# Attention scores in crossed 64x64 tiles by blocks of 64, the causal mask added in PSUM, and the value product in two blocks per half

## The chip, the cores and the metric

One core of a Trainium2 chip runs the whole program. The metric is the device time of one execution in microseconds, lower is better; the time given for a kernel is the median of its runs.

## What is computed

The input is 16 sequences of 512 tokens with 128 features. Three layers follow one another: a mixture of experts, an attention layer, and the same mixture of experts again. Only the attention layer changes here:

```python
q = (x @ Wq + bq).reshape(Bb, Ss, H, HD)      # H = 16 heads of HD = 8
k = (x @ Wk + bk).reshape(Bb, Ss, H, HD)
v = (x @ Wv + bv).reshape(Bb, Ss, H, HD)
scores = jnp.einsum('bthd,bshd->bhts', q, k) / jnp.sqrt(jnp.asarray(HD, x.dtype))
scores = scores + alibi[None]
scores = jnp.where(causal[None, None], -jnp.inf, scores)
attn = jax.nn.softmax(scores, axis=-1)
out = jnp.einsum('bhts,bshd->bthd', attn, v).reshape(Bb, Ss, Dd)
return out @ Wo + bo
```

Here x is layer-normalised first, and the result is added to it.

## The kernel before

**Stages.** `macaron` runs `moe_layer`, `attention` and `moe_layer`. In `attention` each engine has its own program, and all of them follow one order, written out in `walk` (L773): a step b handles sequence b, and at the same time takes the maxima of sequence b+1, the projections of b+2 and the normalisation of b+3. Steps run from -3 to 16; `all_steps` (L763) writes steps -3 to 1 and 12 to 16 out and puts steps 2 to 11 into a loop of two steps each. Step -1 takes maxima only, and step 15 has no maxima.

**Operands.** q and k are split into bf16 parts and stacked, so that one head is 64 rows of `q_st` and `k_st`: head parts, rows for the position term, a row that carries the shift (minus the maximum) and rows that build the mask. A pair of heads (a side a and a side b) fills the rows 0 to 63 and 64 to 127.

**A step before.** It has four groups g of four heads each, all of one side of a half (half `g // 2`, side `g % 2`), and a group has 11 places n:

- *Max unit* (`take_max_scores`, L871): the scores of 128 queries of one head (or of 2 or 4 heads, where few keys lie ahead) against the keys up to them, in one of three PSUM banks `max_ps`. L884 makes the far keys (51 rows deep) and L887 the diagonal block of 128 keys with the mask (64 rows deep). VectorE's `find_max` (L1093) reduces each bank to `neg_max`. A bank is used again when its reduction is done.
- *Exp unit* (`take_exp_scores`, L906, 10 a group): the transposed scores, 128 keys by the queries from them on, in one of three banks `exp_ps`. They lie in the other row half than the max unit's. ScalarE's `exponentiate` (L986) writes `probs`, of which there are two.
- *Mask* (L1058): GpSimd sets the forbidden quarter of `probs` to zero, 4 instructions a group.
- *Values* (`weigh_values`, L922): after places 3, 5, 7 and 9 the products of the previous group's `probs` with v, for keys 0, 1, 2 and 3 of 128, four heads in four column quarters of `pv_ps`, in float32. After the second group of a half, ScalarE copies `pv_ps` to `oT` (L997).
- *Side work*, all through one bank `side_ps`, each waiting until the one before is read: project_q, project_k (L937), project_v (L941), turn_h (L935), the shifts (L947), turn_o0 and turn_o1 (L961, then the divisions on VectorE, L1143 and L1145), turn_o (L952) and output (L955, added on VectorE, L1135). ScalarE copies q and k (L1010); VectorE copies v (L1127).

Where the side work stands is a table by group and place:

```python
SIDE_WORK = [
    {2: "project_q", 4: "shift_hi", 8: "project_k"},
    {1: "turn_o1", 6: "project_v"},
    {1: "turn_o", 6: "shift_lo", 10: "output"},
    {1: "turn_o0", 8: "turn_h"},
]
PV_AFTER = {3: 0, 5: 1, 7: 2, 9: 3}
```

The SP queue stores the parts of q and k (L827), stacks them (L835, L841; the first half waits for the exponentials of the first half two sequences earlier) and places the shifts (L848).

Of the kernel before, what the change touches and what calls it, by code (L numbers as in the profile page):

```python
# [19 lines left out]
P = 128  # L20
# [24 lines left out]
GROUPS = H // 4  # L45
# [21 lines left out]
class Consts:  # L67


    def __init__(self, nc, ctx):  # L70
# [5 lines left out]
        b16 = np.concatenate([bf16_parts(a, 1)[0] for a in (eye, before, np.ones((P, P)))], axis=1)  # L76
# [19 lines left out]
        self.ones_b = b[:, 2 * P:3 * P]  # L96

# [31 lines left out]
def moe_layer(nc, tag, x, consts, Wr, We, x_in=None, out=None, ahead=None):  # L129
# [7 lines left out]
    with ExitStack() as ctx:  # L137
# [289 lines left out]
        def _(dve):  # L427
# [131 lines left out]
            for e in (2, 3):  # L559
# [6 lines left out]
    {2: "project_q", 4: "shift_hi", 8: "project_k"},  # L566
    {1: "turn_o1", 6: "project_v"},
    {1: "turn_o", 6: "shift_lo", 10: "output"},
    {1: "turn_o0", 8: "turn_h"},
# [3 lines left out]
PREPARE = {(0, 5): "split_q0", (0, 6): "split_q1", (0, 7): "split_q2", (0, 8): "split_q3",  # L573
           (0, 10): "split_k0", (1, 0): "split_k1", (1, 1): "split_k2", (1, 2): "split_k3", (2, 5): "add_bias"}
NORMALISE = {(2, 0): "statistics", (2, 1): "aggregate", (2, 2): "add_eps", (2, 3): "take_root", (2, 7): "shift_mean",
             (2, 8): "normalise0", (2, 9): "normalise1", (2, 10): "normalise2", (3, 0): "normalise3"}
PV_AFTER = {3: 0, 5: 1, 7: 2, 9: 3}
MAX_UNITS = 11
EXP_UNITS = 10
MASK_UNITS = 4  # L580

def max_unit(n):

    return [(3, [0]), (3, [1]), (3, [2]), (3, [3]), (2, [0]), (2, [1]), (2, [2]), (2, [3]),
            (1, [0, 1]), (1, [2, 3]), (0, [0, 1, 2, 3])][n]  # L590


def exp_unit(n):

    if n < 4:
        return [(n, 0, 0)]
    if n < 8:
        return [(n - 4, 1, 0), (n - 4, 3, 3 * P)]
    return [(2 * (n - 8), 2, 0), (2 * (n - 8) + 1, 2, 2 * P)]


class AttentionOperands:


    def __init__(self, nc, ctx, consts, Wq, bq, Wk, bk, Wv, bv, Wo, bo):
# [11 lines left out]
        self.v = [sb(f"v{i}", [P, T, PAIRS, 2, VW]) for i in range(2)]  # L617
# [20 lines left out]
    def set_v(self, pool):  # L638

        for i in range(2):  # L640
            self.nc.gpsimd.memset(self.v[i][:], 0.0).then_inc(self.v_set, 1)
        pool.wait_ge(self.v_set, 2)
        for i in range(2):
            for ab in range(2):
                one = ab * VS + HD
                self.nc.gpsimd.memset(self.v[i][:, :, :, ab, one:one + 1], 1.0).then_inc(self.v_set, 1)


def attention(nc, x, consts, ops):
# [12 lines left out]
    with ExitStack() as ctx:  # L662
# [21 lines left out]
        neg_max = both(lambda i: sb(f"neg_max{i}", [P, 2, 2, PAIRS // 2, T], BF16))  # L684
        shift = sb("shift", [T * H // 2, P], BF16)
        probs = both(lambda i: sb(f"probs{i}", [P, EXP_UNITS, S]))
# [27 lines left out]
        SHIFT_DMAS = 1  # L714
# [4 lines left out]
        masked = sem("masked")  # L719
# [5 lines left out]
        NM, NE, NK = GROUPS * MAX_UNITS, GROUPS * EXP_UNITS, GROUPS * MASK_UNITS  # L725
        HALVES = GROUPS // 2

# [45 lines left out]
        def walk(b, par, half, on_max=None, on_exp=None, on_pv=None, on_side=None, on_prepare=None):  # L773

            for g in range(GROUPS):
                for n in range(MAX_UNITS):
                    if on_max and there(b + 1):
                        on_max(b + 1, 1 - par, half + par, g, n)
                    if on_exp and n < EXP_UNITS and there(b):
                        on_exp(b, par, half, g, n)  # L780
                    if on_prepare and (g, n) in PREPARE and there(b + 2):
                        on_prepare(b + 2, par, half + 1, PREPARE[g, n])
                    if on_prepare and (g, n) in NORMALISE and there(b + 3):
                        on_prepare(b + 3, 1 - par, half + par + 1, NORMALISE[g, n])
# [36 lines left out]
        def _(sp):  # L821
# [22 lines left out]
            def place_shift(b, par, half, hf):  # L844

                sp.wait_ge(side_read, use(b if hf else b - 1, "shift_hi" if hf else "shift_lo"))
                pairs = slice(hf * PAIRS // 2, (hf + 1) * PAIRS // 2)
                sp.dma_start(q_st[par][SHIFT_ROW:SHIFT_ROW + SIDE + 1:SIDE, pairs, :],  # L848
                             shift[:]).then_inc(shift_in[par][hf], DMA)
# [16 lines left out]
        def _(pe):  # L866
            def take_max_scores(b, par, half, g, n):

                i, heads = max_unit(n)
                m = g * MAX_UNITS + n  # L870
                if n == 0 and g in (0, 2):  # L871

                    pe.wait_ge(stack_in[par][g // 2], half * (STACK_DMAS * DMA) + STACK_DMAS * DMA)
# [5 lines left out]
                width = (i + 1) * P  # L879
                half_at, ab = g // 2, 1 - g % 2  # L880
                for c, hh in enumerate(heads):
                    r, at, low = 4 * half_at + hh, c * width, ab * SIDE
                    if i > 0:
                        nc.tensor.matmul(max_ps[m % RING][:, at:at + width - P],  # L884
                                         q_st[par][low:low + FAR_ROW, r, i * P:(i + 1) * P],
                                         k_st[par][low:low + FAR_ROW, r, 0:width - P], start=True, stop=True)
                    mm = nc.tensor.matmul(max_ps[m % RING][:, at + width - P:at + width],  # L887
                                          q_st[par][low:low + SIDE, r, i * P:(i + 1) * P],
                                          k_st[par][low:low + SIDE, r, width - P:width], start=True, stop=True)
                mm.then_inc(max_out, 1)  # L890

            def take_exp_scores(b, par, half, g, n):

                m = g * EXP_UNITS + n
                if n == 0 and g in (0, 2):

                    pe.wait_ge(shift_in[par][g // 2], half * (SHIFT_DMAS * DMA) + SHIFT_DMAS * DMA)
# [5 lines left out]
                low = (g % 2) * SIDE  # L903
                for hh, j, c in exp_unit(n):
                    r = 4 * (g // 2) + hh
                    mm = nc.tensor.matmul(exp_ps[m % RING][:, c:c + S - j * P],  # L906
                                          k_st[par][low:low + FINE_ROW, r, j * P:(j + 1) * P],
                                          q_st[par][low:low + FINE_ROW, r, j * P:S], start=True, stop=True)
                mm.then_inc(exp_out, 1)

            def weigh_values(b, par, g, j):

                half_at, ab = divmod(g, 2)
                if j == 0:
                    pe.wait_ge(masked, b * NK + (g + 1) * MASK_UNITS)
                    if ab == 0 and (g > 0 or after(b, 0)):
                        pe.wait_ge(pv_read, b * HALVES + half_at)
                    if g == 0:
                        pe.wait_ge(side_read, use(b - 1, "project_v"))
                for hh in range(4):  # L920
                    n, c = next((n, c) for n in range(EXP_UNITS) for h, jj, c in exp_unit(n) if (h, jj) == (hh, j))
                    mm = nc.tensor.matmul(pv_ps[VW * hh:VW * (hh + 1), j * P:S], v[par][:, j, 4 * half_at + hh, ab, :],  # L922
                                          probs[g % 2][:, n, c:c + S - j * P], start=(ab == 0 and j == 0),
                                          stop=(ab == 1 and j == T - 1))
                if j == T - 1:
                    mm.then_inc(pv_out, 1)

            def side(b, par, half, what):
# [10 lines left out]
                elif what == "project_v":  # L939
                    for t in range(T):  # L940
                        mm = nc.tensor.matmul(side_ps[:, t * P:(t + 1) * P], hT[1 - par][:, t * P:(t + 1) * P],  # L941
                                              w["wv"][:], start=True, stop=True)
                elif what in ("shift_lo", "shift_hi"):
# [3 lines left out]
                    mm = nc.tensor.transpose(side_ps[0:T * H // 2, 0:P // 2].bitcast(BF16),  # L947
# [28 lines left out]
        def _(act):  # L976
            def exponentiate(b, par, half, g, n):
                m = g * EXP_UNITS + n
                act.wait_ge(exp_out, b * NE + (m + 1))
                if n == 0:  # L980

                    if g >= 2:
                        act.wait_ge(pv_out, b * GROUPS + (g - 1))
                    elif after(b, 0):
                        act.wait_ge(pv_out, (b - 1) * GROUPS + (g + 3))
# [204 lines left out]
```

## Time and profile before

| | us |
|---|---|
| median of 3 runs | 921.04 |
| lowest and highest run | 917.84, 2506.57 |
| span of the profiled execution, first to last instruction | 917.2 |
| TensorE matmul busy | 828.9 (90%) |
| VectorE busy | 748.5 (82%) |
| ScalarE busy | 641.5 (70%) |
| GpSimd busy | 539.3 (59%) |

The profiled execution's time is given by its span; what lies around the span is at least what the lowest run has over it, 0.6 us. A busy time holds the whole length of an instruction, so two that follow each other closely overlap in it. Matmuls overlap most: each shows some 0.17 us beyond the streaming of its columns. L12 is line 12 of the kernel. An arrow in a wait points to what ended it.

### The profile page before, as it was taken

The page shows a single profiled execution, that of the slowest core. Times are in us where ns is not written, and L with a number is a line of the kernel's source. Part 1 is how long each engine was busy: PE and PEld are TensorE (multiplying, and loading weights), DVE is VectorE, ACT ScalarE, POOL GpSimd, SP SyncE. Part 2 cuts the span into 40 slices and gives each one's busy share as a digit, 9 for nine tenths or more (in the row PEclk, how much of TensorE's full clock was granted, in tenths as well). Part 3 has the DMA queues.
Part 4 walks back from the last instruction along what each step waited for, and adds up shares of the span by engine and source line. Part 5 has one row for each costly group of instructions (what it writes and reads, how often), then busy time and mean ns, then how long its engine had stood idle before and what let it go on. Part 6 is the DMA issues. An engine that isn't in the chain of part 4 may idle for free. (4 is left out here: it accounts for less than half of the span.)

```text
span 917.2 us, 23978 instructions
## 1 busy us (share of the span) xinstructions
PE 828.9 (90%) x6498; PEld 383.5 (42%) x6498; DVE 748.5 (82%) x2534; ACT 641.5 (70%) x1538; POOL 539.3 (59%) x838
## 2 busy tenths in 40 slices
PE   4999998279899999999999999999999986999997
PEld 2454553033344444434444444443444334544453
DVE  4999998348888988988988988988989504999996
ACT  3777776113778778778778778877877863777775
POOL 3788888332664565565565465475463322788887
PEclk9999999555999999999999999999999995999999
DMA  6500000232232232232232132132131001010101
GB/s 171 105 0 0 0 0 1 77 134 76 97 109 85 90 116 85 80 123 85 70 132 86 62 134 89 63 127 104 60 118 37 2 1 24 24 34 23 34 25 45
DMA packets 57044, 62.50 MB, mean 68 GB/s; under 512 B 6752, under 2 KB 50656, under 8 KB 56864
## 3 DMA queue, kind: packets, MB, share of 16 engines
q1 hardware_dynamic: 56992, 61.86, 20.8%
q8 instruction: 26, 0.43, 0.2%
q14 instruction: 26, 0.21, 0.1%
HBM read 32.23 MB, written 29.36 MB: 67 GB/s over the span
## 5 line engine op out<-in xcount | busy, mean ns | idle before, releaser
L1093 DVE TENSOR_REDUCE att_neg_max<-att_max 128x1 bf16<-128x512 f32 (+3 forms) x704 | 414.1, 636 | 61.0 <-PE att_max L887 58.7
L986 ACT ACTIVATE att_probs<-att_exp 128x512 f32<-128x512 f32 x640 | 357.6, 596 | 100.7 <-PE att_exp L906 96.9
L1058 POOL TENSOR_SCALAR_AFFINE_SELECT att_probs<-att_probs 128x512 f32<-128x512 f32 x256 | 159.1, 635 | 239.2 <-ACT att_probs L986 239.1
L906 PE MATMUL att_exp<-att_q_st,att_k_st 53*128 53x512 bf16 (+3 forms) x1024 | 223.0, 302 | 0.6 <-ACT att_probs L986 0.6
L884 PE MATMUL att_max<-att_k_st,att_q_st 51*128 51x384 bf16 (+2 forms) x768 | 191.3, 285 | 19.3 <-DVE att_neg_max L1093 11.3
L922 PE MATMUL att_pv<-att_probs,att_v 128*32 128x512 f32 (+3 forms) x2048 | 191.3, 446 | 2.7 <-POOL att_probs L1058 2.4
L359 ACT ACTIVATE moe_scaled<-moe_hi,moe_gates 128x128 f32<-128x128 f32 x512 | 145.8, 370 | 65.7 <-PE moe_hi L306 62.8
L887 PE MATMUL att_max<-att_k_st,att_q_st 64*128 64x128 bf16 x1024 | 176.1, 224 | 0.0
L519 DVE SCALAR_TENSOR_TENSOR x<-moe_lo,moe_gates,x 128x128 f32 (+1 forms) x512 | 159.9, 338 | 13.1 <-PE moe_lo L300 12.2
L884 PEld LDWEIGHTS att_max<-att_k_st,att_q_st 51*128 51x128 bf16 x768 | 71.1, 95 | 215.9 <-DVE att_neg_max L1093 160.5
L300 PE MATMUL moe_lo<-moe_we,moe_hT 128*128 128x512 f32 x256 | 135.2, 610 | 0.0
L306 PE MATMUL moe_hi<-moe_we,moe_hT 128*128 128x512 f32 x256 | 132.5, 599 | 0.0
L396 POOL TENSOR_TENSOR moe_part<-moe_scaled 128x256 f32<-128x256 f32 x128 | 94.1, 735 | 35.9 <-ACT moe_scaled L359 31.8
L887 PEld LDWEIGHTS att_max<-att_k_st,att_q_st 64*128 64x128 bf16 x1024 | 88.0, 97 | 12.1 <-issue 11.7
L306 PEld LDWEIGHTS moe_hi<-moe_we,moe_hT 128*128 128x128 f32 x256 | 49.2, 192 | 62.3 <-issue 58.5
L906 PEld LDWEIGHTS att_exp<-att_q_st,att_k_st 53*128 53x128 bf16 x1024 | 65.2, 94 | 11.6 <-ACT att_probs L986 8.6
L410 POOL TENSOR_TENSOR x<-x,moe_part 128x128 f32 (+1 forms) x128 | 58.6, 458 | 12.6 <-DVE x L519 12.5
L337 ACT ACTIVATE moe_hn<-x,moe_nmr,moe_rstd 128x128 f32 (+1 forms) x128 | 52.7, 492 | 17.1 <-DVE moe_nmr L453 17.0
L922 PEld LDWEIGHTS att_pv<-att_probs,att_v 128*32 128x32 f32 x2048 | 40.9, 108 | 53.1 <-issue 42.4
L403 POOL TENSOR_TENSOR moe_part<-moe_part 128x128 f32<-128x128 f32 x128 | 58.2, 455 | 0.2
L300 PEld LDWEIGHTS moe_lo<-moe_we,moe_hT 128*128 128x128 f32 x256 | 44.3, 193 | 31.6 <-issue 21.5
L389 POOL TENSOR_TENSOR moe_rstd<-moe_veps,f_consts 128x4 f32<-128x4 f32 x32 | 32.5, 1017 | 41.2 <-DVE moe_veps L448 38.4
(81 smaller groups left out, 866.1 us busy)
## 6 DMA issues: line engine op xcount, KB each, us to landing
qk_parts<-att_parts SPq DMA_DIRECT2D x32, 384.0 KB, 2.8
att_q_st<-qk_parts SPq DMA_DIRECT2D x64, 192.0 KB
att_k_st<-qk_parts SPq DMA_DIRECT2D x64, 192.0 KB
qk_parts<-att_parts SPq DMA_DIRECT2D x32, 256.0 KB, 2.1
x<-in_L_attn_x SPq DMA_DIRECT2D x16, 256.0 KB, 2.8
qk_parts<-att_parts SPq DMA_DIRECT2D x32, 128.0 KB, 1.7
out<-x SPq DMA_DIRECT2D x16, 256.0 KB, 2.3
moe_we<-in_L_ffn_We SPq DMA_DIRECT2D x2, 512.0 KB, 4.6
```

The lines of the kernel that those rows point to most:

```text
L300: nc.tensor.matmul(lo_ps[t][:], hT[par][:, t * P:(t + 1) * P], we[:, 0:HE, :], start=True, stop=True).then_inc(lo_out, 1)
L306: nc.tensor.matmul(hi_ps[t % 2][:], hT[par][:, t * P:(t + 1) * P], we[:, HE:E, :], start=True, stop=True).then_inc(hi_out, 1)
L359: ins = nc.scalar.activation(scaled[t % 2][:, e, :], hi_ps[t % 2][:, e, :], ACT.Copy, scale=gates[par][:, t, HE + e:HE + e + 1])
L396: nc.gpsimd.tensor_tensor(part2[t % 2][:], scaled[t % 2][:, 0:2, :], scaled[t % 2][:, 2:4, :], ALU.add).then_inc(part_step, 1)
L519: nc.vector.scalar_tensor_tensor(out=xt(b, t), in0=lo_ps[t][:, e, :], scalar=gates[par][:, t, e:e + 1], in1=xt(b, t), op0=ALU.mult, op1=AL ...
L884: nc.tensor.matmul(max_ps[m % RING][:, at:at + width - P], q_st[par][low:low + FAR_ROW, r, i * P:(i + 1) * P], k_st[par][low:low + FAR_ROW ...
L887: mm = nc.tensor.matmul(max_ps[m % RING][:, at + width - P:at + width], q_st[par][low:low + SIDE, r, i * P:(i + 1) * P], k_st[par][low:low ...
L906: mm = nc.tensor.matmul(exp_ps[m % RING][:, c:c + S - j * P], k_st[par][low:low + FINE_ROW, r, j * P:(j + 1) * P], q_st[par][low:low + FIN ...
L922: mm = nc.tensor.matmul(pv_ps[VW * hh:VW * (hh + 1), j * P:S], v[par][:, j, 4 * half_at + hh, ab, :], probs[g % 2][:, n, c:c + S - j * P], ...
L986: nc.scalar.activation(probs[g % 2][:, n, :], exp_ps[m % RING][:], ACT.Exp).then_inc(exp_done, 1)
L1058: nc.gpsimd.affine_select(out=view, in_=view, compare_op=ALU.is_ge, fill=0.0, base=0, pattern=[[0, 4], [1, P]], channel_multiplier=-1).the ...
L1093: nc.vector.tensor_reduce(neg_max[par][:, g // 2, 1 - g % 2, heads[0]:heads[0] + len(heads), i], max_ps[m % RING][:, 0:len(heads) * width] ...
```

## The change

The attention stage goes over from blocks of 128 to blocks of 64. A unit holds both heads of a pair. The max scores of side a use the array's rows 0 to 63 and write partitions 0 to 63, those of side b rows 64 to 127 and partitions 64 to 127. The exponent's scores are crossed: side a writes partitions 64 to 127, side b 0 to 63. A step has two halves of 22 places; a half has 22 max units, 18 exp units and two value blocks. The mask is a further matmul into the exponent's bank, the identity times a constant with -2^100 above the diagonal. One value matmul has both sides' 64 keys as its 128 rows, with the sides' values in different columns of v, so that there are 8 key blocks for 4. `probs` exists once. The value blocks stand at places 4 and 14, which have no exp unit. ScalarE copies v instead of VectorE, GpSimd's mask is gone, the shift is placed by two DMAs instead of one, and all steps are written out. The columns of Wv are reordered on the host, as those of Wq and Wk were.

```diff
+BLOCK = P // 2
+NB = S // BLOCK
+HALVES = 2
+HP = PAIRS // HALVES
...
 SIDE_WORK = [
+    {2: "project_q", 4: "shift_hi", 9: "turn_o1", 12: "project_k", 14: "turn_o", 17: "output", 21: "project_v"},
+    {4: "shift_lo", 9: "turn_o0", 14: "turn_h"},
 ]
...
+PREPARE = {(0, 5): "split_q0", (0, 6): "split_q1", (0, 8): "split_q2", (0, 10): "split_q3",
+           (0, 15): "split_k0", (0, 17): "split_k1", (0, 18): "split_k2", (0, 20): "split_k3", (1, 3): "add_bias"}
+NORMALISE = {(1, 0): "statistics", (1, 1): "aggregate", (1, 2): "add_eps", (1, 5): "take_root", (1, 7): "shift_mean",
+             (1, 8): "normalise0", (1, 9): "normalise1", (1, 10): "normalise2", (1, 11): "normalise3"}
+MAX_UNITS = 22
+EXP_UNITS = 18
+EXP_AT = {n + n // 4: n for n in range(16)} | {20: 16, 21: 17}
+PV_AT = {4: 1, 14: 0}
+PV_UNITS = [(0, 8), (8, 18)]
+PV_KEYS = [[0, 1, 7], [2, 6, 3, 5, 4]]
...
 def max_unit(n):
+    if n < 16:
+        return 7 - n // 4, [n % 4]
+    if n < 20:
+        return 3 - (n - 16) // 2, [2 * (n % 2), 2 * (n % 2) + 1]
+    return 21 - n, [0, 1, 2, 3]
...
 def exp_unit(n):
     if n < 4:
         return [(n, 0, 0)]
+    if n < 16:
+        j = n // 4
+        return [(n % 4, j, 0), (n % 4, NB - j, S - j * BLOCK)]
+    return [(2 * (n - 16), 4, 0), (2 * (n - 16) + 1, 4, S // 2)]
...
-            for b in range(-3, 2):
-                step(b, b % 2, b // 2)
-            with eng.Fori(1, NSEQ // 2 - 2) as i:
-                step(2 * i, 0, i)
-                step(2 * i + 1, 1, i)
-            for b in range(NSEQ - 4, NSEQ + 1):
+            for b in range(-3, NSEQ + 1):
                 step(b, b % 2, b // 2)
...
                     if i > 0:
+                        for low in (0, SIDE):
+                            nc.tensor.matmul(max_ps[m % RING][low:low + BLOCK, at:at + before_block],
+                                             q_st[par][low:low + FAR_ROW, r, before_block:width],
+                                             k_st[par][low:low + FAR_ROW, r, 0:before_block], start=True, stop=True)
+                    for low in (0, SIDE):
+                        mm = nc.tensor.matmul(max_ps[m % RING][low:low + BLOCK, at + before_block:at + width],
+                                              q_st[par][low:low + SIDE, r, before_block:width],
+                                              k_st[par][low:low + SIDE, r, before_block:width], start=True, stop=True)
...
+                for hh, j, c in parts:
+                    r = HP * hf + hh
+                    for low in (0, SIDE):
+                        out_at = SIDE - low
+                        nc.tensor.matmul(bank[out_at:out_at + BLOCK, c:c + S - j * BLOCK],
+                                         k_st[par][low:low + FINE_ROW, r, j * BLOCK:(j + 1) * BLOCK],
+                                         q_st[par][low:low + FINE_ROW, r, j * BLOCK:S], start=(c == 0), stop=False)
+                for low in (0, SIDE):
...
+                    mm = nc.tensor.matmul(blocks[:, 0:step_to * len(parts) - step_to + 1:step_to, :],
+                                          consts.ident_b[low:low + BLOCK, low:low + BLOCK], rows,
+                                          start=False, stop=True)
...
+                pe.wait_ge(exp_done, b * NE + (hf * EXP_UNITS + PV_UNITS[k][1]))
...
+                for j in PV_KEYS[k]:
+                    for hh in range(HP):
+                        n, c = exp_place(hh, j)
+                        mm = nc.tensor.matmul(pv_ps[VW * hh:VW * (hh + 1), j * BLOCK:S], v[par][:, j, HP * hf + hh, :],
+                                              probs[:, n, c:c + S - j * BLOCK], start=(j == 0),
+                                              stop=(j == PV_KEYS[-1][-1]))
...
+                    for j in range(NB):
+                        for ab in range(2):
+                            low = (1 - ab) * BLOCK
+                            mm = nc.tensor.matmul(side_ps[low:low + BLOCK, j * BLOCK:(j + 1) * BLOCK],
+                                                  hT[1 - par][:, j * BLOCK:(j + 1) * BLOCK],
+                                                  w["wv"][:, ab * BLOCK:(ab + 1) * BLOCK], start=True, stop=True)
```

## Rows read from the trace of the kernel before

**Rows 1.** Windows: two steps, step -1, step 15; busy PE, PEld, DVE, ACT, POOL; clock.
```profile
439.17:472.87 33.70, 32.24 (x346) 14.37 (x342) 29.46 (x61) 26.79 (x52) 19.15 (x27) 1.00 0.28 94
607.72:641.17 33.45, 31.89 (x344) 14.10 (x342) 29.46 (x61) 26.72 (x52) 18.98 (x27) 1.00 0.27 94
190.50:222.30 31.80, 28.99 (x132) 12.48 (x132) 26.42 (x56) 3.88 (x8) 9.34 (x10) 0.50 0.32 117
721.90:749.00 27.10, 24.91 (x213) 9.21 (x213) 3.22 (x7) 23.09 (x45) 10.07 (x17) 1.00 0.01 2
```

**Rows 2.** Waits: engine, line, what ended the wait; total us, times, longest.
```profile
PEld att_max L884 <- DVE att_neg_max L1093: 160.5, 326, 1.5
...
DVE att_neg_max L1093 <- PE att_max L887: 58.7, 122, 7.5
```

**Rows 3.** Order in time, VectorE, first group of a step (start, length, idle before).
```profile
424.73 1.88 DVE L1093 TENSOR_REDUCE att_neg_max<-att_max 128x1 bf16<-128x512 f32 x3
426.98 0.69 DVE L1093 TENSOR_REDUCE att_neg_max<-att_max 128x1 bf16<-128x512 f32 x1 [0.38 <-PE att_max L887]
428.25 1.05 DVE L1093 TENSOR_REDUCE att_neg_max<-att_max 128x1 bf16<-128x384 f32 x2 [0.57 <-PE att_max L887]
429.85 1.02 DVE L1093 TENSOR_REDUCE att_neg_max<-att_max 128x1 bf16<-128x384 f32 x2 [0.55 <-PE att_max L887]
```

**Rows 4.** Order in time, TensorE, the same step (start, length).
```profile
425.18 0.38 PE L906 MATMUL att_exp<-att_q_st,att_k_st 53*128 53x512 bf16 x1
425.27 0.22 PE L887 MATMUL att_max<-att_k_st,att_q_st 64*128 64x128 bf16 x1
425.50 1.12 PE L937 MATMUL att_side<-att_hT,att_wq 128*128 128x512 f32 x2
426.55 0.33 PE L884 MATMUL att_max<-att_k_st,att_q_st 51*128 51x384 bf16 x1
...
426.73 0.22 PE L887 MATMUL att_max<-att_k_st,att_q_st 64*128 64x128 bf16 x1
426.88 1.07 PE L922 MATMUL att_pv<-att_probs,att_v 128*32 128x512 f32 x8
427.88 0.28 PE L884 MATMUL att_max<-att_k_st,att_q_st 51*128 51x256 bf16 x1
...
433.80 0.66 PE L961 MATMUL att_side<-f_consts,att_oT 128*128 128x128 f32 x4 [0.16 <-ACT att_oT L997]
434.39 0.33 PE L884 MATMUL att_max<-att_k_st,att_q_st 51*128 51x384 bf16 x1
...
437.88 1.16 PE L941 MATMUL att_side<-att_wv,att_hT 128*128 128x128 f32 x8
```

**Rows 5.** Groups by shape: reductions (busy us, mean ns, idle before).
```profile
L1093 DVE TENSOR_REDUCE att_neg_max<-att_max 128x1 bf16<-128x512 f32 x256 | 165.3, 681 | 15.5 <-PE att_max L887 15.5
...
L1093 DVE TENSOR_REDUCE att_neg_max<-att_max 128x1 bf16<-128x384 f32 x256 | 131.6, 552 | 20.8 <-PE att_max L887 18.7
```

**Rows 6.** Order in time, VectorE, the same step's third and fourth group.
```profile
442.70 0.86 DVE L1104 BATCH_NORM_STATS2 att_bn<-x 128x6 f32 x4
443.48 0.68 DVE L1093 TENSOR_REDUCE att_neg_max<-att_max 128x1 bf16<-128x512 f32 x1
...
450.21 0.69 DVE L1135 TENSOR_TENSOR x<-att_side,x 128x512 f32 x1 [0.24 <-PE att_side L955]
450.82 1.28 DVE L1093 TENSOR_REDUCE att_neg_max<-att_max 128x1 bf16<-128x512 f32 x2
452.01 0.35 DVE L1143 RECIPROCAL att_rden<-att_side 128x32 f32<-128x32 f32 x1
...
452.73 3.33 DVE L1093 TENSOR_REDUCE att_neg_max<-att_max 128x1 bf16<-128x512 f32 x6
```

**Rows 7.** Groups by shape: ScalarE's copy of k and GpSimd's masks.
```profile
L1010 ACT ACTIVATE att_qk<-att_side,att_bk_col 128x512 f32<-128x512 f32 x16 | 11.0, 687 | 11.9 <-PE att_side L937 11.8
...
L1058 POOL TENSOR_SCALAR_AFFINE_SELECT att_probs<-att_probs 128x512 f32<-128x512 f32 x256 | 159.1, 635 | 239.2 <-ACT att_probs L986 239.1
```

More of the change, by code:

```diff
@@ L75, in __init__ @@
         before = (i[:, None] < i[None, :]).astype(np.float64)
-        b16 = np.concatenate([bf16_parts(a, 1)[0] for a in (eye, before, np.ones((P, P)))], axis=1)
+        half = i % BLOCK
+        ahead = np.where(half[:, None] > np.arange(BLOCK)[None, :], -(2.0 ** 100), 0.0)
+        b16 = np.concatenate([bf16_parts(a, 1)[0] for a in (eye, before, np.ones((P, P)), ahead)], axis=1)
         f32 = np.ascontiguousarray(np.concatenate([eye, number, np.full((P, T), -0.5, np.float32)], axis=1))
@@ L565 @@
 SIDE_WORK = [
[L566 to L569, printed above, removed]
-]
[L573 to L580, printed above, removed]
-def max_unit(n):
-    return [(3, [0]), (3, [1]), (3, [2]), (3, [3]), (2, [0]), (2, [1]), (2, [2]), (2, [3]),
-            (1, [0, 1]), (1, [2, 3]), (0, [0, 1, 2, 3])][n]
+    {2: "project_q", 4: "shift_hi", 9: "turn_o1", 12: "project_k", 14: "turn_o", 17: "output", 21: "project_v"},
+    {4: "shift_lo", 9: "turn_o0", 14: "turn_h"},
+]
+PREPARE = {(0, 5): "split_q0", (0, 6): "split_q1", (0, 8): "split_q2", (0, 10): "split_q3",
[8 more added lines that the diff above has]
+PV_KEYS = [[0, 1, 7], [2, 6, 3, 5, 4]]
+NPV = len(PV_UNITS)
+def max_unit(n):
+    if n < 16:
[3 more added lines that the diff above has]
+    return 21 - n, [0, 1, 2, 3]
 def exp_unit(n):
@@ L911, in weigh_values @@
[L911 to L918, printed above, removed]
-                        pe.wait_ge(side_read, use(b - 1, "project_v"))
[L920 to L926, printed above, removed]
+                bank = exp_ps[m % RING]
@@ L999, in side @@
             def side(b, par, half, what):
-                if what in ("project_v", "output", "turn_o0", "turn_o1"):
+                if what in ("output", "turn_o0", "turn_o1"):
                     return
                 act.wait_ge(turned, use(b, what))
-                if what == "turn_h":
+                if what == "project_v":
+                    if after(b, 0):
+                        act.wait_ge(pv_out, (b - 1) * NV + NV)
+                    for ab in range(2):
+                        low = (1 - ab) * BLOCK
+                        ins = nc.scalar.activation(
+                            v[1 - par][low:low + BLOCK, :, :, ab * VS:ab * VS + HD].rearrange("p j r c -> p (j r) c"),
+                            side_ps[low:low + BLOCK, :].rearrange("p (n c) -> p n c", c=HD), ACT.Copy)
+                    ins.then_inc(side_read, 1)
+                elif what == "turn_h":
                     nc.scalar.activation(hT[1 - par][:], side_ps[:], ACT.Copy).then_inc(side_read, 1)
@@ L1045, in _ @@
         def _(pool):
-            def mask(b, par, half, g, n):
-                if n not in (3, 7, EXP_UNITS - 1):
-                    return
-                pool.wait_ge(exp_done, b * NE + (g * EXP_UNITS + n + 1))
-                pool.sem_inc(pool_passed, 1)
-                group = probs[g % 2][:].rearrange("p n (a c) -> p n a c", c=P)
-                if n == EXP_UNITS - 1:
-                    views = [group[:, 8:10, 0:3:2, :].rearrange("p n a c -> p (n a) c")]
-                else:
-                    views = [group[:, n - 3:n + 1, a, :] for a in ((0,) if n == 3 else (0, 3))]
-                for view in views:
-                    nc.gpsimd.affine_select(out=view, in_=view, compare_op=ALU.is_ge, fill=0.0, base=0,
-                                            pattern=[[0, 4], [1, P]], channel_multiplier=-1).then_inc(masked, 1)
             def prepare(b, par, half, what):
```

163 lines of the change are left out of this document (77 added, 86 removed).

## Prediction

> **What bounds the kernel now.** I read four views. The change is all in the attention stage, so first the windows over single steps: a step (one sequence) lasts 33.70 us, and in it TensorE shows 32.2 us busy, VectorE 29.5, ScalarE 26.8, GpSimd 19.2, at a granted clock of 1.00 [rows 1]. TensorE's figure holds the modelled tails of its matmuls, so it doesn't say that TensorE is the bound. Second, the waits: TensorE's weight loads for the max scores wait 160.5 us for VectorE's reductions, and those wait 58.7 us for TensorE [rows 2]. Each waits for the other: three banks lie between them, so whoever falls three units behind stops the other. Third, VectorE's order in time: reductions run back to back until TensorE does something else, then VectorE stands for 0.38, 0.57 and 0.55 us [rows 3]. Fourth, TensorE's order in time shows what it does there: project_q from 425.50 to 426.55, a block of probabilities times values from 426.88 to 427.88 [rows 4]. So a step is VectorE's service plus the holes that TensorE's other work tears into it.
>
> VectorE's service: three 512-column reductions last 1.88 us and one 0.681, so each takes (1.88 - 0.68)/2 = 0.60 us; two of 384 last 1.02 and one 0.552, so 0.47 [rows 3, 5]. That is 1.04 ns a column and 0.065 us fixed. A group has 4 x 0.60 + 4 x 0.465 + 3 x 0.605 = 6.07 us, four groups 24.3. The rest: the addition of the output 0.61 (450.21 to 450.82), the copy of v, of the same size, 0.61, two divisions of 0.72 (452.01 to 452.73), statistics 0.78 (442.70 to 443.48) with three small ones of some 0.5 [rows 6]. Together 28.2, so 5.5 us of the 33.70 are holes.
>
> **The change part by part.** *Reductions:* still 44 a step, but narrower. A half has 4 each of 512, 448, 384 and 320 columns, 2 of 512, 2 of 384, one of 512, one of 256: 11.07 us by the line above, 22.1 a step, 2.15 less. The copy of v goes to ScalarE: 0.61 less. VectorE's service is 25.45.
>
> *ScalarE:* 36 exponentials of 512 instead of 40, and two copies of v over 64 partitions. The nearest row is the 0.69 us copy of k [rows 7]; I take 0.5 each (bounds 0.3 and 0.7). ScalarE has 7 us to spare a step [rows 1], so nothing on the path. *GpSimd* loses its masks, 159.1 us in all [rows 7]; it bounds nothing, and their wait ahead of the products goes only at the very end. Its splits of k, moved later, are done about 14 us into a step, before the stacking DMA that waits for the first half's exponentials; the second shift DMA has some 14 us until its scores start. Nothing.
>
> *Scores.* A max unit is now two matmuls side by side (64 rows by 64 columns each) instead of one of 128 columns, and the exponent's two lie in the other two quarters. The width streamed is that of the unit as before, 0.42 ns a column (0.38 us against 0.22 for 512 and 128 columns [rows 4]). What no row shows is whether the four quarters run at once. The bounds are nothing and twice the time. Row halves do: the exponent's matmul at 425.18 starts before the diagonal max matmul that the program issues ahead of it (425.27), so each row half keeps its own order. Column quarters do: eight value matmuls of 512 columns, two passes each, end within 1.00 us [rows 4]. I take nothing, the nearer rows. The mask's matmuls add 64 or 128 columns behind the exponent's, 0.03 to 0.05 us, hidden while VectorE's unit takes 0.40 to 0.60; ahead of a block they count.
>
> The Trainium skill (TensorE: Matmul & The Clock Gate, section "The mechanism" of Part 3) says that matmuls start and end strictly in program order. The two rows above don't agree: 425.18 precedes 425.27. By that rule the exponent's matmul would follow the far max matmul; rival B is its price.
>
> *Values.* 18,432 columns a step instead of 20,480, in 4 blocks instead of 16. The 512-column block took 1.00 us to the next score (1.07 busy less a tail of 0.17 and 0.05 of filling is 0.85 of streaming; 0.15 is switching) with 0.10 ahead of it (426.73 plus 0.05 to 426.88) [rows 4]. Four heads run abreast, so a block of 1,280 columns (keys 2, 6, 3, 5, 4) is 2.13 + 0.14 = 2.27 us, one of 1,024 is 1.85. TensorE spends 2 x (2.27 + 1.85) + 4 x 0.1 = 8.6 us a step on them instead of 20,480/2,048 x 0.85 + 16 x 0.25 = 12.5. But a block of 1.0 us hides behind the two or three units that VectorE has in hand, and one of 2.3 does not. That decides. The projection of v becomes 16 matmuls of 64 columns in two column halves for 4 of 128, whose eight passes take 1.16 us now [rows 4]: 1.1 again, with 0.6 (halves abreast, weights hidden) and 2.3 (each pass as long as now) as bounds.
>
> *The new order, followed slot by slot.* Rules, each from rows: a reduction starts 0.20 after its matmul has streamed (426.73 + 0.05 to 426.98); a bank is free 0.135 after the 0.60 service; 0.10 passes before a switch; q or k takes 1.05, four transposes 0.59 (433.80 to 434.39), output and v 1.1 [rows 3, 4]. Check on the kernel before: q starts 0.77 after unit 0's reduction (424.73 to 425.50); the rules give 0.72. First half, from unit 0's reduction at 0, VectorE's holes:
> - after unit 2, q (0.72 to 1.78): unit 3 at 2.20 instead of 1.80, 0.40 (before: 0.38).
> - after unit 4, shift_hi and the 2.27 block: TensorE back at 4.74, unit 5 at 5.13 where VectorE was free at 3.33, 1.80.
> - turn_o1 after unit 9 fits. k waits for VectorE's division (8.51), runs to 9.57: 0.19.
> - turn_o waits until ScalarE has copied k (10.51), then the 1.85 block to 12.95; unit 15 at 13.28, VectorE free at 10.70: 2.58.
> - output after unit 17: 0.25. v after unit 21, to 17.82: 0.60.
>
> That is 5.8 of holes and 12.4 of service, 18.2 us. Second half: shift_lo and the long block after unit 4 (2.42 to 4.85): 1.12. turn_h waits for normalise3 (10.1), then the short block to 12.54: unit 15 at 12.87, VectorE free at 10.70: 2.17. With 13.1 of service 16.4 us. A step takes 34.6, 0.9 more than now: service falls by 2.75, holes grow from 5.5 to 9.1.
>
> *Unrolling.* The steps already unrolled take 33.45 instead of 33.70 [rows 1]: 10 steps x 0.25 = -2.5. *Ends.* The step that only takes maxima, 31.80 us at half clock [rows 1], has no value blocks and loses the service alone, -2.7. The one without maxima, 27.10 us [rows 1], loses 4 of 40 exponentials, about -2; the last blocks wait for no mask, about -1. Sum: 15 steps x 0.9 - 2.5 - 5.7 = +5.3 us. The profiled execution's span is 917.2; with the 0.6 us to the lowest run (917.84) around it, it lies 3 below the median of the runs shown, 921.04. On the median: 926.
>
> **The rivals.** *A, faster: the holes don't grow.* TensorE spends 3.9 us a step less on values, and the first score after a block comes at full speed. If VectorE stands 5.5 us as now, a step is 30.95: 15 x -2.75 - 8.2 = -49, 872. For it: the switches saved. Against it: a hole is the block less some 0.9 us in hand, and each block has more than doubled. It decides if blocks start while VectorE has three units, or 1.5 us, left.
>
> *B, slower: max and exponent scores of a row half go one after the other.* A slot with both then streams 352 + 512 columns on average, 0.36 to 0.40 us instead of 0.27. Behind VectorE's 0.5 that hides, but each of ten stops in a step starts some 0.15 later, and the narrow slots 15 to 21 lose 0.3 a half: 2 us a step, 15 x 2 = +30, 956. For it: the queue of a row half is in order, and both now share one. Against it: value matmuls in one row range pass each other. It decides from the first slot with both.
>
> *C, much slower: the two matmuls of a unit exclude each other.* They write one bank, in different partitions and from different row halves, which no row shows. With the max pair in one bank beside the exponent's pair in another, TensorE streams twice 22,528 columns, 18.8 us a step, and 8.6 of values, 7.9 of the rest and some 2 of waits make 37.3 or more: 15 x 3.6 - 8 = +46, 967; with all four in turn 15.4 us more a step, about 1,200.
>
> The Trainium skill (TensorEngine Tiling (Array Packing), section "Gotcha 1: PSUM Pressure") says that different row tiles can't access the same PSUM bank at once. No run here shows it; by that rule C holds.
>
> **How the numbers follow.** My forecast 0.5, A 0.21, B 0.17, C 0.12. About 2% can be told from no change here, 902.6 to 939.5. The forecast's step is good to 1 us, so 926 +- 15: of its 0.5, 0.04 faster, 0.36 same, 0.10 slower. A: 0.18 faster, 0.03 same. B: 0.03 same, 0.14 slower. C: 0.12 slower. Faster 0.22, same 0.42, slower 0.36. The range leaves out the outer half of A and most of C, and so runs from 882 to 985; the forecast's own is 911 to 941.
>
> **What would show it.** A step of about 34.6 us, from one output addition to the next; four holes of VectorE of 1.1 to 2.6 us, each behind a value block, and 25.4 us of service between them. Value blocks of some 2.2 and 1.8 us. In the order of time, a max matmul and an exponent's matmul of one slot starting within 0.03 us; if the second starts only when the far one has streamed, B; if the two max matmuls of a unit start a stream apart, C. If the reduction behind a value block starts within 1 us of the one before it, A. The clock below 1.00 in full steps would make all of it wrong.

## The result and the profile after

The changed kernel takes 931.53 us (median of 4 runs, 930.01 to 934.25) beside 919.44 for the kernel before on the same chip: a ratio of 1.0131, 95% interval 1.0102 to 1.0160. It is 1.3% slower: more than the spread of the runs, and inside the 2% that the forecast counts as no change. One of the four runs of the kernel before took 2506.57 us; the median of the other three is 917.84, and by it the change costs 1.5%. The forecast was 926.0. The profiled execution's span is 930.1 us, 12.9 more than the 917.2 of before.

Two full steps of the kernel after, by windows (length, busy PE, PEld, DVE, ACT, POOL, clock, DMA share, GB/s); they answer to [rows 1]. The third row is the step that only takes maxima, the fourth the first step with both, the last the 14 steps behind it, up to the start of their last reduction (the last two of them are shorter, in both kernels):

```profile
443.26:478.21 34.95, 31.04 (x636) 19.07 (x638) 26.05 (x60) 24.96 (x50) 9.35 (x11) 1.00 0.28 94
478.21:513.16 34.95, 31.04 (x636) 19.07 (x638) 26.05 (x60) 24.96 (x50) 9.36 (x11) 1.00 0.28 94
...
191.42:221.24 29.82, 26.83 (x289) 14.23 (x289) 23.75 (x54) 5.06 (x10) 9.32 (x10) 0.56 0.34 121
221.24:253.44 32.20, 28.83 (x580) 16.57 (x576) 24.57 (x56) 23.78 (x48) 9.34 (x10) 0.95 0.23 77
...
253.44:737.40 483.96, 430.61 (x8810) 265.18 (x8804) 361.71 (x805) 344.24 (x688) 120.57 (x129) 1.00 0.27 90
```

The same three stretches of the kernel before:

```profile
190.53:222.29 31.76, 28.95 (x132) 12.47 (x132) 26.41 (x55) 3.88 (x8) 9.34 (x10) 0.50 0.32 118
222.29:256.65 34.36, 30.42 (x294) 11.99 (x292) 27.82 (x58) 25.49 (x50) 18.85 (x26) 0.90 0.20 71
...
256.65:722.18 465.53, 446.67 (x4774) 197.56 (x4773) 408.96 (x820) 368.63 (x716) 257.25 (x353) 1.00 0.26 91
```

Every engine does less in a full step (VectorE 26.05 us for 29.46, GpSimd 9.35 for 19.15, TensorE 31.04 for 32.24), and yet it takes 34.95 us for 33.70. The 14 steps cost 18.4 us more, the two in front of them 1.9 and 2.2 less.

The waits of the kernel after (total us, times, longest) show where the saved work went:

```profile
DVE att_neg_max L1119 <- PE att_max L904: 143.1, 122, 9.5
...
PEld att_max L900 <- DVE att_neg_max L1119: 77.2, 162, 1.5
```

In [rows 2] TensorE waited 160.5 us for VectorE and VectorE 58.7 for TensorE. The sides have changed.

VectorE's order in time, one step (start, length, in brackets the idle time before and what ended it), only the rows with a hole and, first, the addition of the output that begins the step; it answers to [rows 3]:

```profile
443.26 0.69 DVE L1153 TENSOR_TENSOR x<-att_side,x 128x512 f32<-128x512 f32 x1
...
446.44 0.69 DVE L1119 TENSOR_REDUCE att_neg_max<-att_max 128x1 bf16<-128x512 f32 x1 [0.62 <-PE att_max L904]
...
451.61 1.69 DVE L1119 TENSOR_REDUCE att_neg_max<-att_max 128x1 bf16<-128x448 f32 x3 [1.05 <-PE att_max L904]
...
459.31 3.55 DVE L1119 TENSOR_REDUCE att_neg_max<-att_max 128x1 bf16<-128x320 f32 x7 [2.17 <-PE att_max L904]
463.12 1.89 DVE L1119 TENSOR_REDUCE att_neg_max<-att_max 128x1 bf16<-128x512 f32 x3 [0.26 <-PE att_max L904]
465.17 1.22 DVE L1119 TENSOR_REDUCE att_neg_max<-att_max 128x1 bf16<-128x512 f32 x2 [0.17 <-PE att_max L904]
...
468.31 2.62 DVE L1119 TENSOR_REDUCE att_neg_max<-att_max 128x1 bf16<-128x448 f32 x5 [1.91 <-PE att_max L904]
...
473.12 0.89 DVE L1119 TENSOR_REDUCE att_neg_max<-att_max 128x1 bf16<-128x320 f32 x2 [0.15 <-PE att_max L904]
...
476.42 1.69 DVE L1119 TENSOR_REDUCE att_neg_max<-att_max 128x1 bf16<-128x320 f32 x3 [2.40 <-PE att_max L904]
```

446.44 is unit 0 of a second half, 463.12 unit 0 of the next first half: the halves take 16.68 and 18.27 us. The four big holes (1.05, 2.17, 1.91, 2.40) each stand behind a value block; 0.62 stands behind project_v, 0.17 behind project_q, 0.15 behind project_k.

TensorE's order in time in the same step; it answers to [rows 4]:

```profile
448.88 2.38 PE L951 MATMUL att_pv<-att_probs,att_v 128*32 128x384 f32 x40
451.18 0.35 PE L900 MATMUL att_max<-att_k_st,att_q_st 51*64 51x384 bf16 x2
451.19 0.38 PE L926 MATMUL att_exp<-att_q_st,att_k_st 53*64 53x448 bf16 x2
451.37 0.19 PE L904 MATMUL att_max<-att_k_st,att_q_st 64*64 64x64 bf16 x2
...
457.08 1.93 PE L951 MATMUL att_pv<-att_probs,att_v 128*32 128x512 f32 x24
458.94 0.30 PE L900 MATMUL att_max<-att_k_st,att_q_st 51*64 51x256 bf16 x2
```

The long block runs 2.30 us to the next score (448.88 to 451.18), the short one 1.86. The row of 451.18 and that of 451.19 are four matmuls, two for a max unit and two for an exponent's, and all four start within 0.02 us.

### The profile page after: what moved, and what is told of

The parts are those of the page before. It is cut to its first block and busy times, and to the rows that moved or that the text cites. A ratio compares the mean times of both kernels' runs of the same rounds, so it can differ in the third digit from the quotient of the medians.

```text
span 930.1 us, 30329 instructions
## 1 busy us (share of the span) xinstructions
PE 806.2 (87%) x11106; PEld 460.4 (50%) x11106; DVE 695.5 (75%) x2518; ACT 613.5 (66%) x1506; POOL 383.4 (41%) x582
## 3 DMA queue, kind: packets, MB, share of 16 engines
HBM read 32.24 MB, written 29.36 MB: 66 GB/s over the span
## 5 line engine op out<-in xcount | busy, mean ns | idle before, releaser
L1119 DVE TENSOR_REDUCE att_neg_max<-att_max 128x1 bf16<-128x512 f32 (+6 forms) x704 | 371.9, 588 | 143.1 <-PE att_max L904 143.1
L900 PE MATMUL att_max<-att_k_st,att_q_st 51*64 51x448 bf16 (+6 forms) x1792 | 196.2, 288 | 43.3 <-DVE att_neg_max L1119 34.6
L926 PE MATMUL att_exp<-att_q_st,att_k_st 53*64 53x512 bf16 (+7 forms) x2048 | 201.3, 291 | 5.1 <-ACT att_probs L1017 4.3
L900 PEld LDWEIGHTS att_max<-att_k_st,att_q_st 51*64 51x64 bf16 x1792 | 93.6, 108 | 131.8 <-DVE att_neg_max L1119 77.2
L904 PE MATMUL att_max<-att_k_st,att_q_st 64*64 64x64 bf16 x2048 | 154.2, 195 | 4.8 <-DVE att_neg_max L1119 4.8
L951 PE MATMUL att_pv<-att_probs,att_v 128*32 128x512 f32 (+7 forms) x2048 | 137.8, 408 | 1.0 <-ACT att_probs L1017 1.0
L935 PE MATMUL att_exp<-bf_consts 64*64 64x128 bf16 (+1 forms) x1152 | 125.0, 212 | 0.0
L402 POOL TENSOR_TENSOR moe_part<-moe_scaled 128x256 f32<-128x256 f32 x128 | 94.1, 735 | 34.6 <-ACT moe_scaled L365 31.7
L904 PEld LDWEIGHTS att_max<-att_k_st,att_q_st 64*64 64x64 bf16 x2048 | 101.6, 109 | 8.7 <-DVE att_neg_max L1119 7.8
L926 PEld LDWEIGHTS att_exp<-att_q_st,att_k_st 53*64 53x64 bf16 x2048 | 82.1, 106 | 15.7 <-ACT att_probs L1017 12.2
L312 PEld LDWEIGHTS moe_hi<-moe_we,moe_hT 128*128 128x128 f32 x256 | 49.2, 192 | 62.3 <-issue 58.7
L935 PEld LDWEIGHTS att_exp<-bf_consts 64*64 64x64 bf16 x1152 | 64.3, 106 | 11.6
```

The source lines that it names most:

```text
L312: nc.tensor.matmul(hi_ps[t % 2][:], hT[par][:, t * P:(t + 1) * P], we[:, HE:E, :], start=True, stop=True).then_inc(hi_out, 1)
L402: nc.gpsimd.tensor_tensor(part2[t % 2][:], scaled[t % 2][:, 0:2, :], scaled[t % 2][:, 2:4, :], ALU.add).then_inc(part_step, 1)
L900: nc.tensor.matmul(max_ps[m % RING][low:low + BLOCK, at:at + before_block], q_st[par][low:low + FAR_ROW, r, before_block:width], k_st[par] ...
L904: mm = nc.tensor.matmul(max_ps[m % RING][low:low + BLOCK, at + before_block:at + width], q_st[par][low:low + SIDE, r, before_block:width], ...
L926: nc.tensor.matmul(bank[out_at:out_at + BLOCK, c:c + S - j * BLOCK], k_st[par][low:low + FINE_ROW, r, j * BLOCK:(j + 1) * BLOCK], q_st[par ...
L935: mm = nc.tensor.matmul(blocks[:, 0:step_to * len(parts) - step_to + 1:step_to, :], consts.ident_b[low:low + BLOCK, low:low + BLOCK], rows ...
```

## The experiments

The theory: a step is VectorE's service plus holes, and a value block tears a hole (leaves VectorE idle) by what it lasts beyond the two or three reductions that the three banks hold, so a few long blocks cost more than many short ones. Its rivals: TensorE's load as such sets the step; the crossed tiles don't run abreast; the two matmuls of a unit exclude each other.

**Shorter blocks.** Five value blocks a half instead of two, none above 512 columns, at their own places. The same columns are streamed; with the length of the blocks their places change too.

```diff
-PV_AT = {4: 1, 14: 0}
-PV_UNITS = [(0, 8), (8, 18)]
-PV_KEYS = [[0, 1, 7], [2, 6, 3, 5, 4]]
+PV_AT = {4: 4, 7: 0, 11: 1, 16: 2, 20: 3}
+PV_UNITS = [(0, 4), (4, 8), (8, 12), (12, 16), (16, 18)]
+PV_KEYS = [[0], [1, 7], [2, 6], [3, 5], [4]]
+LATE = {4}
...
```

> The changed kernel with its two value blocks per half cut into five (keys 0; 1 and 7; 2 and 6; 3 and 5; 4) at places 7, 11, 16, 20 and, for the last, 4 of the next half; nothing else moves. If a step is VectorE's service plus holes that grow with the length of a block beyond the 0.9 us of reductions in hand, the holes of 1.9, 2.5, 1.1 and 2.2 us give way to ten of 0.2 to 0.6 us, a step falls from 34.95 to about 32 us, and the time to about 885 us. If TensorE's total work bounds a step, six more switches of 0.25 us make it longer: about 36.4 us a step, 953 us.

Measured: 908.75 us, ratio to the kernel before 0.9853 [0.9770, 0.9936]. The direction is the theory's, and the rival, by which TensorE's total bounds every step, is gone. The size is not the theory's: the step takes 33.30 us where about 32 was expected. The windows of this kernel over a first half, then a second half:

```profile
452.45:470.71 18.26, 17.34 (x347) 10.13 (x347) 13.28 (x27) 12.93 (x25) 8.35 (x9) 1.00 0.41 134
470.71:485.75 15.04, 13.35 (x293) 7.29 (x285) 13.37 (x34) 12.44 (x27) 1.02 (x1) 1.00 0.17 55
```

The second half fell from 16.68 to 15.04 us. The first stayed at 18.26, where it was 18.27. It holds the projections of q, k, v and the output, and TensorE's 17.34 us busy leave 0.9. VectorE's order in time shows what happened to its holes:

```profile
462.31 0.89 DVE L1120 TENSOR_REDUCE att_neg_max<-att_max 128x1 bf16<-128x320 f32 x2 [0.97 <-PE att_max L905]
463.75 1.10 DVE L1120 TENSOR_REDUCE att_neg_max<-att_max 128x1 bf16<-128x320 f32 x2 [0.54 <-PE att_max L905]
465.52 0.70 DVE L1120 TENSOR_REDUCE att_neg_max<-att_max 128x2 bf16<-128x512 f32 x1 [0.68 <-PE att_max L905]
...
470.71 0.69 DVE L1120 TENSOR_REDUCE att_neg_max<-att_max 128x1 bf16<-128x512 f32 x1 [1.17 <-PE att_max L905]
```

The big holes of 1.91 and 2.40 us are gone, but the half has nine holes of 0.2 to 1.2 us where it had five, since a block of 1.0 us now stands right ahead of project_k and another just ahead of project_v. So the theory was half of it: holes by block length where TensorE has time to spare, TensorE's own sum where it has none.

**Without the crossing.** The exponent's scores go to the same quarters as the max scores instead of the opposite ones, and v is laid out to match.

```diff
...
-                        out_at = SIDE - low
+                        out_at = low
...
-                            low = (1 - ab) * BLOCK
+                            low = ab * BLOCK
...
```

> The changed kernel with the exponent's scores not crossed: side a writes partitions 0 to 63 and side b 64 to 127, so that the max and the exponent's scores share two quarters of the array and the other two stay empty; v is laid out to match. If the crossing is what lets both kinds run at once, each of ten stops in a step starts some 0.15 us later: about 37 us a step, 960 us (the price that the prediction put on its rival B). If VectorE hides it all: 931 us, no change from the changed kernel.

Measured: 959.83 us, ratio 1.0411 [1.0323, 1.0499]; a step takes 36.72, 1.77 more than in the changed kernel. TensorE's order in time in this kernel:

```profile
474.16 0.38 PE L900 MATMUL att_max<-att_k_st,att_q_st 51*64 51x448 bf16 x2 [0.50 <-DVE att_neg_max L1119]
474.35 0.22 PE L904 MATMUL att_max<-att_k_st,att_q_st 64*64 64x64 bf16 x2
474.38 0.41 PE L926 MATMUL att_exp<-att_q_st,att_k_st 53*64 53x512 bf16 x2
474.60 0.22 PE L935 MATMUL att_exp<-bf_consts 64*64 64x64 bf16 x2
474.63 0.38 PE L900 MATMUL att_max<-att_k_st,att_q_st 51*64 51x448 bf16 x2
```

Max, exponent, max: each pair starts when the one before it has streamed (0.22 us from 474.16 to 474.38, 0.25 to 474.63). That is rival B, made on purpose, and it costs what B was said to cost. In the changed kernel the crossing does what the forecast counted on.

**The kernel before with its four value blocks of a group as one.** This puts blocks of 1,280 columns into the kernel before and leaves its scores, masks and tiles alone.

```diff
-PV_AFTER = {3: 0, 5: 1, 7: 2, 9: 3}
+PV_AFTER = {5: 0}
...
+                        for j in range(T):
...
```

> The kernel before with one part of the change alone: the four value blocks of a group in one, at place 5. By the theory of holes, the block of 2.3 us leaves a hole of 1.8 us in each of four groups, 7.2 us a step where the values cost some 4.2 now: 36.5 us a step, 962 us, although TensorE saves 12 switches of 0.25 us. If TensorE's total bounds a step, those 3 us come off: 30.7 us, 876 us.

Measured: 1022.94 us, ratio 1.1092 [1.0998, 1.1186], a step of 40.97 us. Merging makes it slower and not faster, so rival A's hope (fewer switches and nothing else) falls. The size was missed by more than 4 us a step, and the windows inside a step show why:

```profile
438.00:440.00 2.00, 1.87 (x16) 0.88 (x13) 2.00 (x7) 1.66 (x4) 0.75 (x2) 1.00 0.22 72
440.00:442.00 2.00, 0.93 (x8) 0.42 (x8) 2.00 (x10) 1.38 (x4) 0.64 (x1) 0.56 0.39 135
442.00:446.00 4.00, 4.00 (x28) 1.17 (x28) 1.37 (x3) 0.84 (x2) 2.26 (x2) 0.50 0.25 93
```

The clock falls to 1.2 GHz in the second window: a mean of 0.56 between 1.00 ahead of it and 0.50 behind it puts the fall at some 440.2. TensorE had been busy 1.87 of the 2.00 us before that window, and stood 0.90 us for VectorE when the clock fell. TensorE's and VectorE's order in time there:

```profile
432.04 2.36 PE L923 MATMUL att_pv<-att_probs,att_v 128*32 128x512 f32 x32
...
440.92 0.39 PE L885 MATMUL att_max<-att_k_st,att_q_st 51*128 51x256 bf16 x1 [0.90 <-DVE att_neg_max L1094]
...
442.40 4.50 PE L923 MATMUL att_pv<-att_probs,att_v 128*32 128x512 f32 x32
```

```profile
434.70 0.56 DVE L1094 TENSOR_REDUCE att_neg_max<-att_max 128x1 bf16<-128x384 f32 x1 [1.61 <-PE att_max L888]
...
447.30 1.05 DVE L1094 TENSOR_REDUCE att_neg_max<-att_max 128x1 bf16<-128x384 f32 x2 [3.93 <-PE att_max L888]
...
458.14 4.61 DVE L1094 TENSOR_REDUCE att_neg_max<-att_max 128x1 bf16<-128x384 f32 x8 [3.30 <-PE att_max L888]
...
466.86 1.62 DVE L1094 TENSOR_REDUCE att_neg_max<-att_max 128x1 bf16<-128x384 f32 x3 [2.08 <-PE att_max L888]
```

The block that the forecast's rule puts at 2.27 us takes 4.50, and VectorE stands 3.93 behind it. The same rows separate the two causes. The blocks ahead of 434.70 and 466.86 ran at a granted 1.00, took 2.36 us each and left 1.61 and 2.08, where 1.8 was expected; those ahead of 447.30 and 458.14 ran wholly or in part at 0.50 and left 3.93 and 3.30. So the holes of long blocks are there at full clock, and the two slow ones are 3.6 us longer than expected, most of the miss.

**The kernel before, written out.** All its steps are unrolled, nothing else; the changed kernel is unrolled too.

```diff
-            for b in range(-3, 2):
...
-            with eng.Fori(1, NSEQ // 2 - 2) as i:
...
+            for b in range(-3, NSEQ + 1):
```

> The kernel before with all steps written out instead of ten in a loop, one part of the change alone. The prediction's term: 10 steps of 33.45 instead of 33.70 us, 2.5 us less, about 917 us. The other view: the difference between those steps came from what the late steps no longer have to do, and the loop costs nothing: 919 to 920 us.

Measured: 915.45 us, ratio 0.9952 [0.9932, 0.9972], 4.4 us less. One step, by windows:

```profile
448.70:481.98 33.28, 31.95 (x344) 13.81 (x343) 29.41 (x61) 26.61 (x53) 19.19 (x27) 1.00 0.29 97
```

It takes 33.28 us for 33.70: 0.42 a step over 10 steps, where the forecast had 0.25. The opposite edit, the changed kernel with a loop, wasn't tried.

**Two banks for the max scores.** The changed kernel with one bank less: one reduction less in hand.

```diff
-        max_ps = [ps(f"max{i}", [P, S]) for i in range(RING)]
+        MAX_RING = 2
+        max_ps = [ps(f"max{i}", [P, S]) for i in range(MAX_RING)]
...
```

> The changed kernel with two PSUM banks for the max scores instead of three; nothing else moves. If the holes are what a block lasts beyond the reductions that VectorE still has in its banks, one bank less takes a reduction of 0.4 to 0.6 us out of the cover at each of some nine stops: about 4.5 us a step, and 0.5 more at the narrow units, 34.95 to about 40 us, the time to about 1,005 us. If a step is bounded by TensorE's own work, 931 us.

Measured: 1016.48 us, ratio 1.1046 [1.0990, 1.1101]. Two steps by windows, from the output on and from unit 0 on:

```profile
440.46:481.08 40.62, 33.71 (x636) 19.25 (x638) 26.97 (x60) 25.78 (x50) 9.37 (x11) 0.96 0.25 81
...
504.52:543.45 38.93, 32.03 (x638) 18.46 (x634) 26.97 (x60) 25.77 (x50) 9.37 (x10) 1.00 0.25 84
```

VectorE's order in time in the first, and one row of the second:

```profile
451.82 1.73 DVE L1120 TENSOR_REDUCE att_neg_max<-att_max 128x1 bf16<-128x448 f32 x3 [3.59 <-PE att_max L905]
...
459.91 3.73 DVE L1120 TENSOR_REDUCE att_neg_max<-att_max 128x1 bf16<-128x320 f32 x7 [2.21 <-PE att_max L905]
463.91 1.89 DVE L1120 TENSOR_REDUCE att_neg_max<-att_max 128x1 bf16<-128x512 f32 x3 [0.26 <-PE att_max L905]
466.54 1.22 DVE L1120 TENSOR_REDUCE att_neg_max<-att_max 128x1 bf16<-128x512 f32 x2 [0.74 <-PE att_max L905]
469.68 2.74 DVE L1120 TENSOR_REDUCE att_neg_max<-att_max 128x1 bf16<-128x448 f32 x5 [1.91 <-PE att_max L905]
...
475.62 0.89 DVE L1120 TENSOR_REDUCE att_neg_max<-att_max 128x1 bf16<-128x320 f32 x2 [0.97 <-PE att_max L905]
478.91 1.71 DVE L1120 TENSOR_REDUCE att_neg_max<-att_max 128x1 bf16<-128x320 f32 x3 [2.40 <-PE att_max L905]
```

```profile
531.36 1.73 DVE L1120 TENSOR_REDUCE att_neg_max<-att_max 128x1 bf16<-128x448 f32 x3 [1.91 <-PE att_max L905]
```

Most full steps take 40.6 us; three of the twelve keep the full clock and take 38.9. The rows of 451.82 and 531.36 stand behind the same long block of the second half: 3.59 us where the granted clock was 0.50, 1.91 at 1.00. So of the 5.67 us that a step is longer than the changed kernel's, 1.7 is the clock's and 4.0 the missing bank's.

The missing bank does not cost the same everywhere. Behind that long block the hole grows by 0.86 (1.05 with three banks), behind project_q by 0.57 and behind project_k by 0.82: one reduction or a little more. Behind the other three value blocks it stays (1.91, 2.21 and 2.40 for 1.91, 2.17 and 2.40). Another stop of TensorE is close ahead of each of these: project_q and the wait for its copy, turn_h, or turn_o. When the block begins, VectorE has two units in hand behind the first and none behind the other two, with three banks as with two. The total comes near the expectation, but it was worked out as a reduction at each of some nine stops with no clock in it.

**Moving the projections.** The five-block kernel with project_v taken to the second half, whose TensorE had 1.7 us to spare; and then with the output too, and project_k and turn_o moved on from the value blocks. Both edits are against the changed kernel and hold the five blocks too.

```diff
-    {2: "project_q", 4: "shift_hi", 9: "turn_o1", 12: "project_k", 14: "turn_o", 17: "output", 21: "project_v"},
-    {4: "shift_lo", 9: "turn_o0", 14: "turn_h"},
+    {2: "project_q", 4: "shift_hi", 9: "turn_o1", 12: "project_k", 14: "turn_o", 17: "output"},
+    {4: "shift_lo", 9: "turn_o0", 13: "project_v", 18: "turn_h"},
...
```

> The kernel with five value blocks per half, whose first half still lasts 18.3 us and whose second lasts 15.0, with project_v moved from the first half (place 21) to the second (place 13; turn_h goes to 18 to stay behind it). In that kernel TensorE's pieces add up to some 17 us in the first half and 12 in the second. If the first half is now bounded by TensorE and the second by VectorE, the 1.1 us go out of the first and hide in the second for the most part: a step of about 32.6 instead of 33.3 us, about 898 us. If both halves are bounded by the holes alone, moving a piece moves its hole with it: 33.3 us, 909 us.

```diff
-    {2: "project_q", 4: "shift_hi", 9: "turn_o1", 12: "project_k", 14: "turn_o", 17: "output", 21: "project_v"},
-    {4: "shift_lo", 9: "turn_o0", 14: "turn_h"},
+    {2: "project_q", 4: "shift_hi", 9: "turn_o1", 13: "project_k", 18: "turn_o"},
+    {1: "output", 4: "shift_lo", 9: "turn_o0", 13: "project_v", 18: "turn_h"},
...
```

> As five_v, and the output goes to the second half too (place 1), project_k to place 13 and turn_o to 18, where it no longer waits for ScalarE's copy of k. TensorE's pieces then add up to some 14.7 us in each half, VectorE's service to 11.8 and 13.7. By the same reading about 15.5 us each, a step of 31.0 us, about 875 us. If holes move with their pieces, 33 us and 905 us.

Measured: 895.49 us, ratio 0.9730 [0.9691, 0.9770], a step of 32.50; and 878.45 us, ratio 0.9544 [0.9513, 0.9575], a step of 31.3. The second beats the kernel before by 4.6% and is the fastest here. The largest holes of its step, VectorE's order in time:

```profile
463.62 1.50 DVE L1120 TENSOR_REDUCE att_neg_max<-att_max 128x1 bf16<-128x320 f32 x3 [0.88 <-PE att_max L905]
...
468.33 2.23 DVE L1120 TENSOR_REDUCE att_neg_max<-att_max 128x4 bf16<-128x256 f32 x4 [0.52 <-PE att_max L905]
```

No hole reaches 1 us, and the halves stand at 15.2 and 16.1 us. Both runs came out as the completed theory said, within 0.3 us a step: it is the placing of the same work that decides.

## Why the prediction was near, point by point

*Service and holes.* The profile counts idle time from a reduction's end, 0.08 behind its service (0.68 less 0.60). With that added, the first half's holes are 0.25, 1.99, 0.23, 2.48, 0.18 and 0.70, against 0.40, 1.80, 0.19, 2.58, 0.25 and 0.60: 5.83 together, forecast 5.8. The second half's are 1.13 and 2.25, against 1.12 and 2.17. What is left of the step, 25.4 us, is the forecast's 25.45. The halves were to take 18.2 and 16.4.

*The step that failed.* "Second half ... with 13.1 of service 16.4 us" has no hole ahead of the next half's unit 0, and one of 0.26 (0.34 with the 0.08) is there at 463.12. A step has 44 max units and the ring three banks, and 44 leaves a rest: unit 0 takes the bank of the last unit but one, not the last but two, so TensorE leads by two. The 0.26 stands ahead of unit 0 in each of the 14 steps. With two banks, where TensorE leads by two throughout, it is 0.26 as well (463.91). The forecast's own rules give some 0.2 there: from the release of its bank, unit 0 needs some 0.55 us, and the last reduction, now of 256 columns, covers 0.33 of it. The forecast had run them from unit 0 on and not across the seam. In the full steps of the kernel before, whose last reduction has 512 columns (0.60 us), no hole stands there. The second term is unrolling. The kernel before gains 0.42 a step by it, where "10 steps x 0.25" was put; in the changed kernel, written out, the step is still 0.35 above the 34.6 that the forecast put before that gain. The seam accounts for that 0.35, so no gain shows. That unrolling is worth nothing where VectorE waits for TensorE is only argued.

*The sum.* Forecast for the 14 steps behind the first full one: 14 x 0.9 - 2.5 = +10.1; measured +18.4. Of the 8.3 between them the seam is 4.9 and the missing gain 2.5; the other 0.9 comes from steps of the kernel before that were written out already and were priced at 33.70. The step of maxima alone gave 1.94 of the 2.7 and the end of the stage 1.9 of the 3. The first full step was priced at +0.9 like the others and gave 2.2 back. No sequence is ahead of it, so it has no long block in its first half and no hole of 1.91 there, and its clock is 0.95 where it was 0.90; what each is worth isn't separated. That hid 3.1 us of the miss, by luck. These and 0.5 outside the stage make +12.9 for a forecast of +5.3: right in the mechanism, 7.6 us short, inside the range and inside the likeliest case's own. One reading of [rows 4] is off, and nothing hangs on it: the eight value matmuls of two passes each are four matmuls, and the eight rows are their passes.

*The rivals.* A fell: holes grew. B fell in the changed kernel, and the uncrossed one gives its price, +28.3 us for the +30 that was worked out. C fell on the trace: the two matmuls of a unit write one bank from different row halves and start side by side (451.18). The rule of the Trainium skill that B rested on (TensorE: Matmul & The Clock Gate, "The mechanism" of Part 3: strictly in program order) holds in the uncrossed kernel, where the pairs share their quarters, and not in the changed one, where an exponent's pair of another quarter starts 0.01 us behind the max pair and ahead of that unit's own diagonal (451.19 and 451.37). The rule of the Trainium skill behind C (TensorEngine Tiling (Array Packing), "Gotcha 1: PSUM Pressure": different row tiles not in one bank at once) would forbid the pair at 451.18; the measurement decides.

## What to carry to other kernels

A block on an in-order engine is free as long as its consumer has work in hand, here two or three reductions of 0.4 to 0.6 us; what it lasted beyond that stood here as a hole. So split long blocks down to the cover and keep other stops away from them. Count the cover by what the consumer holds when the block begins and not by the number of banks: taking a bank away cost 0.86 us at one value block and 0.04 or less at the three that another stop had just preceded. Count the engine's work in each half of a period, not only in the whole: the five short blocks paid at once in the half with time to spare, and in the full half only when projections had moved out. A ring whose length doesn't divide the units loses a place at every seam; here a hole opened there when the last unit had become short.

## What the runs showed of the hardware that was not expected

Four matmuls in four quarters of the array ran side by side, each two of them into one PSUM bank at different partitions (all started within 0.02 us); with max and exponent scores sharing quarters a step took 1.77 us longer.

The granted clock fell inside full steps of two kernels whose TensorE had stood waiting for VectorE. In the kernel before with merged blocks it went from 2.4 to 1.2 GHz some 0.2 us into a wait of 0.90 us, and the block behind took 4.50 us where others took 2.36 at 1.00. In the changed kernel with two banks it fell just after the long block of the second half had begun (granted 0.75 in 447.00:448.00, 0.50 behind it); TensorE had been busy 0.50, 0.29 and 0.45 us in the three us before. The slower block then made VectorE's hole longer, 3.59 for 1.91. In the changed kernel itself, with holes on VectorE's side, the full steps stayed at 1.00.
